# Last chunk's chain into attention reordered, its fold done by two products, and the query side of two chunks moved to GpSimd

## The chip, the cores and the metric

One core of a Trainium2 chip runs the whole program. The metric is device time in microseconds (us) of that core. The engines are TensorE (PE in the profile), VectorE (DVE), ScalarE (ACT), GpSimd (POOL) and SyncE (SP), which here only issues DMAs.

## The reference, cut to what matters

Two transformer layers on x of 2048 tokens by 128 features. The stages around the change are the end of layer 0's mixture of experts and the front of layer 1's attention:

```python
# layer 0 feed-forward: a shared expert and 8 gated ones
x = x + shared + selected
# layer 1 attention, on n = layernorm(x)
q_in = linear(n, Wq, bq);  Q = linear(cat(q_in, conv1d(q_in, convq)), qproj)   # kernel of 3 tokens
k_in = linear(n, Wk, bk);  K = linear(cat(k_in, conv1d(k_in, convk)), kproj)
V = linear(n, Wv, bv)
tau   = sigmoid(conv1x1(gelu(depthwise3(n, tau1)), tau2))
delta = sigmoid(conv1x1(gelu(depthwise3(n, del1)), del2))
scores = einsum(Q, K) / sqrt(8) * tau[..., None] + delta[:, :, None, :]
x = x + linear(softmax(scores) @ V, out_w, out_b)        # 16 heads of 8
# layer 1 feed-forward: 8 experts, each token goes to two of them
```

## The kernel before

The 2048 tokens are cut into four chunks of 512 (`RANGE`, for the convolutions; the last has 513 columns). Layer 0 runs a scan over the chunks, and beside it the feed-forward of chunks 0 to 2. `scan_order` is one order of steps, written by hand, that every engine program walks with its own functions: `epilog`, `gates`, `ffn` (36 up-projections, each with its down-projections), `later` (the norm of layer 1), `kside` (keys and delta), `tside` (the depthwise taps of tau) and `qside` (queries, tau and values). A function yields once a step, and `pull(gen, n)` advances it by n steps; so the order of `pull` calls is the order in each engine's queue.

The feed-forward of chunk 3 is the last. Beside its steps run the key, tau and query sides of chunks 0 to 2, and twenty of the "early" units (`EARLY_STEPS`): a unit is two products of queries with 512 keys into two PSUM banks, and one VectorE reduction of both to maxima. Each gated expert's output goes through `gate_expert` (VectorE, `GO`, L1687), then `add` (GpSimd, `FO += GO`, L2091). After expert 8's `add`, TensorE transposes `FO` (L896), and VectorE adds the result into `x_tok` (L1705). Two pulls of `Q2`, the query side of chunk 2, stand at steps 48 and 50, in front of and behind that fold.

Then comes the chain of chunk 3: statistics (VectorE L1507, L1511), `power` (GpSimd, rstd and shift, L2022 to L2032), the scaling of tokens (`scaled`, ScalarE, L1224), transposes (PE L732), the copy to `XN` (ACT L1361), the keys' convolution (PE L948, L951, ACT L1382, L1385) with the depthwise taps of delta (DVE L1751, L1755) and their Gelu (ACT L1405), the gate products (PE L959, L962) and the sigmoid (ACT L1392, L1393). `parts_of` (DVE L1733 to L1741) splits keys, delta or queries into three bf16 parts. These go out to memory and come back in the layout of the score products: keys over `sk` (SP L2414, L2421), delta over `sc` (`delta_out` L661 and `delta_in` L669, for chunk 3 in ScalarE's queue), queries over `sq` (SP L2443).

The remaining units of group 0's maxima are the `first` units (0 to 11, and one of a single key column; PE L1059 and L1051, DVE L1827). Those over the keys of chunk 3 wait for both the keys and delta to have landed. Their negated maxima (DVE L1823) go through `turned` (PE L1082, ACT L1445, five VectorE instructions L1846 to L1854, SP L2449 and L2453) and become three more rows of the queries. `ahead` does `AHEAD` units of group 1 meanwhile (PE L1074, DVE L1836). `meet` is a barrier of all engines.

Behind it `attention_order` runs 16 groups of 32 score units. A unit has two score products (PE L1110), two exponentials (ACT L1474), one unit of maxima for the next group (PE L1074, DVE L1836), and from the fifth on the eight products with the values (PE L1122). Maxima run `LEAD_MAXIMA` = 10 units ahead of the scores: six are done before the barrier, and four stand in front of the first score. VectorE first does `query_parts(3)` there (L1803, then L1733 to L1741).

Of the kernel before, what the change touches and what calls it, by code (L numbers as in the profile page):

```python
# [16 lines left out]
C = 512  # L17
# [59 lines left out]
def scan_order(p):  # L77
# [52 lines left out]
    Q2 = p["qside"](2)  # L130
    for step, _ in enumerate(chain(p["epilog"](3), both(p["gates"](3), p["ffn"](3)))):
# [6 lines left out]
        if step in (48, 50):  # L138
            pull(Q2)
# [3 lines left out]
    L, K, tau, Q = p["later"](3), p["kside"](3), p["tside"](3), p["qside"](3)  # L143
# [79 lines left out]
def nothing(*_):  # L223
# [8 lines left out]
            kside=lambda c: idle(KSIDE), tside=lambda c: idle(TSIDE), qside=lambda c: idle(QSIDE), early=nothing, first=nothing, ahead=nothing, turned=nothing,  # L232
# [23 lines left out]
EARLY_STEPS = (29, 30, 31, 32, 33, 34, 35, 36, 37, 39, 40, 41, 42, 43, 44, 45, 46, 47, 48, 49)  # L256
EARLY = len(EARLY_STEPS)

AHEAD = 6

FIRST = 13 + AHEAD

# [35 lines left out]
def attention_order(p):  # L298
# [88 lines left out]

    for _ in range(LEAD_MAXIMA - AHEAD):
        next_max()
    for G in range(NG):  # L390
# [5 lines left out]
        for h in range(HALVES):  # L396
# [28 lines left out]
def build(nc, A, out):  # L425
    with ExitStack() as ctx:
# [54 lines left out]
        with ExitStack() as ph:  # L481
# [45 lines left out]
            SQ = [sa(f"SQ{i}", [128, C])[:, :] for i in range(2)]  # L527

            pp2, yy2, vv2 = (pp_, GO[0]), (yy, GO[1]), (vv[:, :], FO[:, :])

            ey, vp = (yy, pp_), (vv[:, :], sa("vv1", [128, C])[:, :])
# [194 lines left out]
        def tensor_program(e):  # L726
# [134 lines left out]
            def ffn(tc):  # L861
# [31 lines left out]
                w.wait_ge(S("gated"), 9 * tc + 9)  # L893
                w.wait_ge(S("ffn_sum"), 8 * tc + 8)
                for b in range(4):
                    t = e.transpose(bank(SUM_BANK[tc])[:, 128 * b:128 * b + 128], FO[:, 128 * b:128 * b + 128], ident[:, :])  # L896
# [69 lines left out]
            def kside(c):  # L966
                made(c)
                w.wait_ge(S("gate_d"), c)
                if c == 3:
                    w.wait_ge(S("f_free"), EARLY)  # L970
# [7 lines left out]
                yield from idle(4)  # L978

# [8 lines left out]
            def qside(c):  # L988
# [7 lines left out]
                elif c == 3:  # L996
                    w.wait_ge(S("x_ffn"), 4)
                conv(c, "convq", 1, 0, "mm_convq")
                yield
                if c != 2:  # L1000
                    values(c)
                    yield from idle(2)
                    w.wait_ge(S("v"), 4 * c + 4)
# [1592 lines left out]
```

## Time and profile before

| | us |
|---|---|
| median of 3 runs | 1483.82 (1479.96 to 1485.55) |
| the profiled execution | 1478.26 |
| its span in the profile | 1476.4 |

PE is busy for 1263.8 us of the span, VectorE for 1231.4, ScalarE for 1034.7 and GpSimd for 662.6. The span is from the first to the last instruction, and what lies around it is 1.9 us. A line of a timeline merges equal instructions that follow each other; "idle before" names what ended the wait. Matmuls of four-byte numbers appear as two instructions each, transposes as one.

### The profile page before, as it was taken

How to read it: one execution, taken by the hardware profiler on the slowest of the kernel's cores; microseconds unless marked ns; L12 is line 12 of the kernel's file. 1: busy time of each engine (PE TensorE's matmuls, PEld its weight loads, DVE VectorE, ACT ScalarE, POOL GpSimd, SP SyncE). 2: the span in 40 equal slices, each digit the busy share in tenths (PEclk: the TensorE clock that was granted, in tenths of full speed). 3: DMA queues.
4: the chain of work that ended last, by engine and by line, in shares of the span. 5: the costliest groups of instructions: out<-in, count | busy, mean ns of one | idle time of the engine just before them, and what ended most of it. 6: DMA issues, size and time to landing. Idle time of an engine off the chain costs nothing.

```text
span 1476.4 us, 22824 instructions
## 1 busy us (share of the span) xinstructions
PE 1263.8 (86%) x8424; PEld 498.1 (34%) x8424; DVE 1231.4 (83%) x1574; ACT 1034.7 (70%) x1832; POOL 662.6 (45%) x762
## 2 busy tenths in 40 slices
PE   4645789888977996887479999999999999999996
PEld 2211334333443443333212222222222222223896
DVE  3999988898989874666689999999999999982764
ACT  5541488678836833643249998999989998998654
POOL 1989878977978864624303001200020003430374
PEclk8767889999988998999669999999999999999999
DMA  8222132212322212430222115100010000002023
GB/s 238 83 77 86 57 95 79 85 60 86 93 71 86 88 29 67 101 90 22 45 65 52 31 31 84 23 3 2 2 24 2 2 2 2 20 28 56 19 76 117
DMA packets 83577, 84.15 MB, mean 57 GB/s; under 512 B 15497, under 2 KB 59018, under 8 KB 83466
## 3 DMA queue, kind: packets, MB, share of 16 engines
q1 hardware_dynamic: 80852, 77.47, 19.5%
q0 software_dynamic: 2496, 5.13, 1.0%
q8 instruction: 66, 1.08, 0.3%
q14 instruction: 45, 0.37, 0.1%
q10 hardware_dynamic: 118, 0.10, 0.0%
HBM read 66.45 MB, written 16.23 MB: 56 GB/s over the span
## 4 chain that ended last, share of the span: by engine, by line
PE 49%; DVE 25%; ACT 9%; issue 8%; POOL 7%; DMA 2%; DVEq 0%; ACTq 0%; POOLq 0%; SPq 0%
DVE mx L1836 14%; PE PS L1122 13%; PE PS L1110 7%; PE PS L858 5%; PE PS L1074 5%; PE PS L867 5%; PE PS L810 2%; POOL D L2060 2%; PE PS L1192 2%; DVE D L1613 2%; PE PS L1207 2%; ACT D L1321 1%; DVE PS L1592 1%; ACT L1321 1%; PE PS L776 1%
## 5 line engine op out<-in xcount | busy, mean ns | idle before, releaser
L1474 ACT ACTIVATE aa<-PS 128x512 f32<-128x512 f32 x1024 | 551.8, 598 | 51.2 <-PE PS L1110 41.0
L1836 DVE TENSOR_REDUCE mx<-PS 128x2 f32<-128x1024 f32 x480 | 551.8, 1216 | 10.2 <-PE PS L1074 8.1
L1122 PE MATMUL PS<-aa,D 128*32 128x256 f32 x4096 | 321.9, 392 | 1.5 <-ACT aa L1474 0.6
L1110 PE MATMUL PS<-D 54*128 54x512 bf16 x1024 | 215.8, 390 | 9.4 <-ACT aa L1474 9.4
L1074 PE MATMUL PS<-D 51*128 51x512 bf16 x960 | 194.2, 387 | 15.6 <-DVE mx L1836 13.0
L2168 POOL CAST n<-nm 16x128 bf16<-16x128 f32 x15 | 4.2, 282 | 409.3 <-ACT nm L1456 409.3
L867 PE MATMUL PS<-xnT,f_w 128*128 128x512 f32 x288 | 159.2, 647 | 7.7 <-ACT HB L1348 6.9
L1592 DVE TENSOR_TENSOR_SCAN PS<-PS,D 128x512 f32<-128x512 f32 x128 | 157.5, 1231 | 7.6
L1348 ACT ACTIVATE HB<-PS 128x512 f32<-128x512 f32 x144 | 84.0, 595 | 106.3 <-PE PS L867 99.2
L858 PE MATMUL PS<-HB,f_w 128*128 128x512 f32 x288 | 147.1, 620 | 6.8 <-DVE GO L1687 5.9
L1122 PEld LDWEIGHTS PS<-aa,D 128*32 128x32 f32 x4096 | 84.3, 108 | 195.3 <-issue 153.4
L1321 ACT ACTIVATE D<-D,Am 128x512 f32<-128x512 f32 x128 | 85.1, 714 | 73.9 <-DVE D L1613 71.9
L810 PE MATMUL PS<-D,ident 128*128 128x512 f32 x192 | 107.9, 687 | 32.7 <-POOL D L2067 27.9
L2067 POOL TENSOR_TENSOR D<-D 128x1024 f32<-128x1024 f32 x48 | 113.0, 2354 | 47.6 <-DVE D L1613 47.5
L1110 PEld LDWEIGHTS PS<-D 54*128 54x128 bf16 x1024 | 54.4, 93 | 221.5 <-ACT aa L1474 165.3
L2060 POOL TENSOR_TENSOR D<-D 128x1024 f32<-128x1024 f32 x48 | 113.2, 2358 | 26.6 <-DVE D L1560 23.4
L1613 DVE TENSOR_TENSOR_SCAN D<-D,hl,PS 128x512 f32<-128x512 f32 x96 | 122.6, 1277 | 2.9
L858 PEld LDWEIGHTS PS<-HB,f_w 128*128 128x128 f32 x288 | 57.0, 199 | 82.7 <-issue 70.5
L2304 POOL DMA_INDIRECT ys<-D,idsI x46 | 48.6, 1056 | 77.5 <-DVE D L1981 70.6
L867 PEld LDWEIGHTS PS<-xnT,f_w 128*128 128x128 f32 x288 | 54.5, 203 | 76.0 <-issue 51.7
L810 PEld LDWEIGHTS PS<-D,ident 128*128 128x128 f32 x192 | 39.3, 212 | 91.4 <-issue 51.1
L1605 DVE SCALAR_TENSOR_TENSOR PS<-PS,D 128x512 f32<-128x512 f32 x96 | 66.8, 695 | 2.6 <-POOL D L2060 0.3
(385 smaller groups left out, 1667.1 us busy)
## 6 DMA issues: line engine op xcount, KB each, us to landing
D<-bc SPq DMA_DIRECT2D x128, 256.0 KB, 3.5
GB<-gd SPq DMA_DIRECT2D x32, 256.0 KB, 4.1
D<-sq SPq DMA_DIRECT2D x8, 384.0 KB, 5.6
xs<-zero SPq DMA_DIRECT2D x1, 2944.0 KB, 18.6
f_w<-in_L_ffn_experts_w SPq DMA_DIRECT2D x1, 2048.0 KB, 9.6
f_w<-in_L_ffn_experts_w SPq DMA_DIRECT2D x8, 256.0 KB, 6.1
aa<-in_L_ffn_W SPq DMA_DIRECT2D x8, 256.0 KB, 3.3
D<-in_L_ffn_W SPq DMA_DIRECT2D x8, 256.0 KB, 3.5
```

The costliest lines, as they stand in the source:

```text
L810: e.matmul(bank(g), ident[:, :], wb[k % 4][:, g, :], start=(n == 0), stop=(n == 15)).then_inc(S("mm_sum"), 1)
L858: e.matmul(down_bank(tc, n // 4), f_w2[:, n // 4, n % 4, :], HB1[i % 6], start=(n % 4 == 0), stop=(n % 4 == 3)).then_inc(S("mm_down"), 1)
L867: e.matmul(bank(4 + i % 2), f_w1[:, n // 4, 128 * (n % 4):128 * (n % 4) + 128], XN[:, ts], start=True, stop=True).then_inc(S("mm_up"), 1)
L1074: t = e.matmul(to[:, hh, :], query(hh, qc % 2, p, b), KS[64 * hh:64 * hh + 51, p, 512 * c:512 * c + 512], start=True, stop=True)
L1110: e.matmul(take_exp(s + hh), KS[64 * hh:64 * hh + 54, p, 128 * kb:128 * kb + 128], QP[64 * hh:64 * hh + 54, qc % 2, p, :], start=True, sto ...
L1122: t = e.matmul(PS[32 * j:32 * j + 32, 7, cs], va[:, kb, 9 * h:9 * h + 32], Pt[K % 3][:, 512 * j + 256 * n:512 * j + 256 * n + 256], start= ...
L1321: e.activation(ab[k % 3][:, g, :], DL[tc % 2][:, g, :], ACT.Exp, scale=Am[:, c:c + 1]).then_inc(S("a"), 1)
L1474: e.activation(Pt[K % 3][:, c:c + 512], bank((s + hh) % 3), ACT.Exp).then_inc(S("e_free"), 1)
L1592: e.tensor_tensor_scan(out=bank(3), data0=bank(2), data1=ab[k % 3][:, g, :], initial=0.0, op0=ALU.max, op1=ALU.mult).then_inc(S("sP"), 1)
L1613: e.tensor_tensor_scan(out=pb[k % 2][:, g, :], data0=ab[k % 3][:, g, :], data1=bank(3), initial=hl[:, 16 * g + n:16 * g + n + 1] if tc els ...
L1836: e.tensor_reduce(mx4[:, G % 2, :, pair, b, c:c + 1], max_banks(m), AX.X, ALU.max).then_inc(freed(m)[0], 1)
L2060: e.tensor_tensor(wb[k % 4], DU[tc % 2][:, :, :], Bb[k % 3].unsqueeze(1).to_broadcast([128, 2, C]), ALU.mult).then_inc(S("wB"), 1)
```

## The change

- Fold: for chunk 3 the last `add` is gone. TensorE multiplies `FO` (which holds experts 0 to 7) and then `GO[0]` (expert 8) by the identity, both into one bank.
- Norm of chunk 3: GpSimd makes rstd alone, and VectorE subtracts and scales in place of ScalarE.
- Order: the query side of chunk 2 leaves the feed-forward's steps and is spread over the chain of chunk 3 (`third`). Early units are 18, at steps 29 to 46, and the `first` units are 15.
- Keys and delta of chunk 3 (`keys`): the Gelu comes before the evacuation of the convolution, both depthwise taps before the parts, and no `first` unit stands between the parts of the keys and those of delta. GpSimd's taps for tau wait until the parts of delta are done. Each key part goes out as soon as it is made; of the keys that come back, the first two of eight rows of heads (`0:2`) come first, and the other six (`2:8`) once delta has gone out.
- `query_parts` of chunks 2 and 3 are now GpSimd's `last`, behind the barrier; so are their DMAs.
- `AHEAD` is 4; the other six units of the lead are spread over the first six score units. A one-column exponential on ScalarE stands at the barrier.

```diff
     drain(sgen)
     p["collect"](3)
-    Q2 = p["qside"](2)
...
-        if step in (48, 50):
-            pull(Q2)
...
     drain(lgen)
-    L, K, tau, Q = p["later"](3), p["kside"](3), p["tside"](3), p["qside"](3)
+    p["third"]("gelu")
...
+    L = p["later"](3)
     pull(L)
-    pull(Q2)
-    pull(L, 3)
-    pull(Q2)
+    p["third"]("conv")
     drain(L)
-    drain(Q2)
-    pull(K, 2)
-    drain(tau)
-    pull(Q)
-    pull(K)
+    for stage in ("conv", "taps", "gelu", "evac", "gate"):
+        p["keys"](stage)
+    p["third"]("gate")
+    p["third"]("values")
+    for stage in ("parts", "out", "delta", "rest"):
+        p["keys"](stage)
+    drain(p["tside"](3))
+    p["third"]("sums")
     firsts(0, 1)
-    pull(K, 2)
-    pull(Q)
-    firsts(2, 3)
-    drain(K)
-    pull(Q)
-    firsts(4, 5, 6)
-    pull(Q)
-    firsts(7, 8, 9, 10, 11)
-    drain(Q)
-    firsts(12)
+    p["queries"]("conv")
+    firsts(2, 3, 4, 5)
+    p["queries"]("values")
+    p["queries"]("gelu")
+    firsts(6, 7, 8, 9)
+    p["queries"]("gate0")
+    firsts(10, 11)
+    p["queries"]("gate1")
+    firsts(12, 13, 14)
     ahead(0)
     p["turned"]()
     ahead(*range(1, AHEAD))
...
-AHEAD = 6
+AHEAD = 4
...
-    for _ in range(LEAD_MAXIMA - AHEAD):
-        next_max()
...
             next_max()
+            if unit["max"] < t + 1 + LEAD_MAXIMA:
+                next_max()
...
# TensorE, ffn(3): the fold
+                if tc == 3:
+                    w.wait_ge(S("hid"), 144)
+                    for x, (summed, sem, n) in enumerate(((FO, "ffn_sum", 31), (GO[0], "gated", 36))):
+                        w.wait_ge(S(sem), n)
+                        for b in range(4):
+                            t = e.matmul(bank(4)[:, 128 * b:128 * b + 128], summed[:, 128 * b:128 * b + 128], ident[:, :],
+                                         start=(x == 0 and b == 0), stop=(x == 1 and b == 3))
...
# VectorE, later(3)
+                    drain(norm(7, 3, 4, "p"))
+                    w.wait_ge(S("p_tp"), 7)
+                    w.wait_ge(S("p_pw"), 23)
+                    for b in range(4):
+                        e.tensor_scalar(xn1[:, b, :], x_tok[:, 12 + b, :], mv[:, 4 + b, 0:1], rstd[:, 4 + b:5 + b],
+                                        ALU.subtract, ALU.mult).then_inc(S("p_xn"), 1)
...
# ScalarE
+                elif stage == "delta":
+                    delta_out(e, w, 3)
+                    delta_in(e, w, 3)
...
# GpSimd, tside: taps of tau
                     if c == 3:
-                        w.wait_ge(S("t1"), 24)
+                        w.wait_ge(S("d_parts"), 20)
...
+            def last():
+                for c, src, tau, n in ((2, q2, tau2, C), (3, C3[0], tauC, C + 1)):
+                    out_ = [qp[:, k, 0:n] for k in range(3)]
...
+                    e.tensor_scalar(src, src, float(8.0 ** -0.5), None, ALU.mult).then_inc(tau_done, 1)
+                    e.tensor_tensor(src, src, tau, ALU.mult).then_inc(tau_done, 1)
+                    w.wait_ge(S("d_sq"), 48 * c)
+                    e.tensor_copy(out_[0], src).then_inc(done, 1)
+                    e.tensor_tensor(src, src, out_[0], ALU.subtract).then_inc(done, 1)
+                    e.tensor_copy(out_[1], src).then_inc(done, 1)
+                    e.tensor_tensor(src, src, out_[1], ALU.subtract).then_inc(done, 1)
+                    e.tensor_copy(out_[2], src).then_inc(done, 1)
...
# SyncE
+            def keys(stage):
+                if stage == "out":
+                    for k, g, m in ((0, 0, 3), (1, 3, 2), (2, 5, 1)):
+                        w.wait_ge(S("k_parts"), 16 + 2 * k)
...
+                    for hh in range(2):
+                        e.dma_start(KS[64 * hh:64 * hh + 48, 0:2, a:b], rows48(sk, hh, slice(a, b))[:, 0:2]).then_inc(
+                            S("d_key3"), 16)
+                elif stage == "rest":
+                    w.wait_ge(S("d_sd"), 64)
+                    w.wait_ge(S("d_key2"), KEY_ROWS)
+                    for hh in range(2):
+                        e.dma_start(KS[64 * hh:64 * hh + 48, 2:8, a:b], rows48(sk, hh, slice(a, b))[:, 2:8]).then_inc(
+                            S("d_key2"), 16)
...
             def last():
+                query_out(2)
                 query_out(3)
```

The waits inside `last` between its own instructions are left out above. The memsets of the value tiles of chunks 2 and 3 move from `qside(2)` to `qside(1)` on GpSimd, and one transpose of `turned` goes to bank 2.

## Rows read from the trace of the kernel before

**Rows 1.** Windows: us, busy us of each engine (count), granted clock, DMA share, GB/s.

```profile
754.00:760.00 6.00, 5.04 (x18) 1.10 (x18) 5.21 (x6) 5.89 (x11) 0.00 (x0) 0.50 0.76 219
760.00:766.00 6.00, 6.00 (x42) 1.05 (x43) 4.13 (x4) 3.04 (x7) 0.00 (x0) 0.51 0.16 46
1100.00:1200.00 100.00, 97.20 (x1028) 25.62 (x1026) 99.00 (x94) 93.30 (x175) 3.36 (x10) 1.00 0.05 6
```

**Rows 2.** Timeline of PE: start us, us, line, operation, [idle before].

```profile
680.71 1.98 PE L858 MATMUL PS<-HB,f_w 128*128 128x512 f32 x4
682.53 2.74 PE L948 MATMUL PS<-xnT,w_convq 128*128 128x512 f32 x6
...
688.94 0.63 PE L896 MATMUL PS<-ident,FO 128*128 128x128 f32 x4 [1.64 <-POOL FO L2091]
...
692.07 1.16 PE L984 MATMUL PS<-w_Wv,xnT 128*128 128x128 f32 x8 [0.78 <-ACT D L1393]
...
753.33 0.63 PE L1110 MATMUL PS<-D 54*128 54x512 bf16 x2
...
761.99 1.08 PE L1122 MATMUL PS<-aa,D 128*32 128x256 f32 x8
...
763.97 1.08 PE L1122 MATMUL PS<-aa,D 128*32 128x256 f32 x8
```

**Rows 3.** Timeline of DVE, same columns.

```profile
686.78 0.68 DVE L1687 SCALAR_TENSOR_TENSOR GO<-PS,GB 128x512 f32<-128x512 f32 x1
...
691.24 0.38 DVE L1511 BATCH_NORM_AGGREGATE mv<-st 128x2 f32<-128x6 f32 x4
...
738.10 0.24 DVE L1823 TENSOR_REDUCE mxh<-mx 128x16 f32<-128x80 f32 x1
...
741.08 5.73 DVE L1836 TENSOR_REDUCE mx<-PS 128x2 f32<-128x1024 f32 x5
...
747.79 0.43 DVE L1733 CAST D<-D 128x513 bf16<-128x513 f32 x1
...
750.18 0.43 DVE L1741 CAST D<-D 128x513 bf16<-128x513 f32 x1
...
764.08 1.23 DVE L1836 TENSOR_REDUCE mx<-PS 128x2 f32<-128x1024 f32 x1 [0.75 <-PE PS L1074]
```

**Rows 4.** Timeline of POOL.

```profile
687.54 1.26 POOL L2091 TENSOR_TENSOR FO<-FO,GO 128x512 f32<-128x512 f32 x1 [6.75 <-DVE GO L1687]
...
692.34 1.38 POOL L2028 TENSOR_TENSOR rstd<-rstd,mhalf 128x4 f32<-128x4 f32 x1
```

**Rows 5.** Chain that ended last, 690 to 730 us: start us, us, what.

```profile
694.09 1.66 ACT xn L1224 x4
...
697.60 4.54 PE PS L948 x6
...
702.89 0.69 ACT D L1385
...
704.80 1.22 DVE D L1737
...
714.42 6.13 DMA sc<-D
...
721.95 2.89 DMA D<-sc
...
727.51 3.71 PE PS L959 x4
```

**Rows 6.** Groups of DVE by line: busy us, mean ns.

```profile
L1893 DVE TENSOR_SCALAR xn<-x_tok,mv,rstd 128x128 f32<-128x128 f32 x8 | 2.2, 372 | 0.5 <-POOL rstd L2028 0.5
```

**Rows 7.** One line, L661: from issue to landing over its four issues.

```profile
DMA to landing us min/median/max: 3.2/4.5/6.1
```

**Rows 8.** Timeline of the SP queue.

```profile
742.58 0.57 SPq L2453 DMA_DIRECT2D D<-nd  x2
```

**Rows 9.** Groups of POOL by line.

```profile
L2137 POOL TENSOR_SCALAR D<-xnT,t1w 128x512 f32<-128x512 f32 (+2 forms) x16 | 26.3, 1642 | 1.6
```

More of the change, by code:

```diff
@@ L231 @@
             ffn=lambda tc: idle(FFN), later=lambda tc: idle(NORM), combine=lambda: idle(COMBINE), start=nothing,
-            kside=lambda c: idle(KSIDE), tside=lambda c: idle(TSIDE), qside=lambda c: idle(QSIDE), early=nothing, first=nothing, ahead=nothing, turned=nothing,
+            kside=lambda c: idle(KSIDE), tside=lambda c: idle(TSIDE), qside=lambda c: idle(QSIDE), early=nothing, first=nothing, ahead=nothing, turned=nothing, keys=nothing, queries=nothing, third=nothing,
             rows=nothing, mulW=nothing, mulB=nothing, scanX=nothing, scanP=nothing, mulC=nothing, clamp=nothing,
@@ new lines, in queries @@
+            def queries(stage):
+                if stage == "conv":
+                    w.wait_ge(S("mm_convq"), 4)
+                    w.wait_ge(S("q_parts"), 10)
+                    conv(3, 0, 1, 7, "conv_q")
+                elif stage == "gelu":
+                    for g in range(2):
+                        w.wait_ge(S("t2"), 5 * g + 35)
+                        e.activation(TC[g], TC[g], ACT.Gelu).then_inc(S("gelu_t"), 1)
+                elif stage == "gate1":
+                    w.wait_ge(S("mm_gate_t"), 4)
+                    w.wait_ge(S("q_tau"), 2)
+                    gate(3, tauC, 128, cols[:, 6:7], 1, 0, "gate_t")
@@ L1434, in qside @@
                 yield
-                if c != 2:
-                    gelus()
-                    yield from idle(2)
+                for g in range(2):
+                    w.wait_ge(S("t2"), 10 * c + 5 * g + 5)
+                    e.activation(TC[g][:, 0:b - a], TC[g][:, 0:b - a], ACT.Gelu).then_inc(S("gelu_t"), 1)
+                yield from idle(2)
                 w.wait_ge(S("mm_gate_t"), c + 1)
@@ L1784, in qside, with keys, third, queries @@
                 yield from idle(3)
-                if c < 3:
-                    query_parts(c)
+                query_parts(c)
                 yield
                 yield
+            def keys(stage):
+                if stage == "taps":
+                    w.wait_ge(S("mm_gate_d"), 3)
+                    taps(3, 0)
+                    taps(3, 1)
+                elif stage == "parts":
+                    w.wait_ge(S("conv_k"), 4)
+                    w.wait_ge(S("d_sk"), 144)
+                    parts_of(C3[1], kp, C + 1, S("k_parts"), 15)
+                elif stage == "delta":
+                    w.wait_ge(S("gate_d"), 4)
+                    w.wait_ge(S("d_sd"), 48)
+                    parts_of(delC, dp, C + 1, S("d_parts"), 15)
+            def third(stage):
+                if stage == "sums":
+                    values(2)
+            def queries(stage):
+                if stage == "values":
+                    values(3)
             def values(c):
@@ L1857, in vector_program @@
                                    epilog=epilog, gates=gates, ffn=ffn, later=later, combine=combine, kside=kside, qside=qside,
-                                   early=early, first=first, ahead=lambda j, m: maxima(1, j, m), turned=turned))
+                                   early=early, first=first, ahead=lambda j, m: maxima(1, j, m), turned=turned, keys=keys,
+                                   queries=queries, third=third))
             meet(e, w)
@@ L1868, in turn @@
                 w.wait_ge(S("m_full"), m + 1)
+                w.wait_ge(S("rs"), 1)
                 if G:
@@ L2101, in ffn @@
                 yield
-                add(8)
+                if tc < 3:
+                    add(8)
                 yield
```

204 lines of the change are left out of this document (136 added, 68 removed).

## The prediction

> **What bounds the kernel now.** I read the windows of the attention stage first. Far from its edges VectorE is busy for 99.0 of 100 us and TensorE for 97.2 [rows 1]: both are full, TensorE takes new maxima only when VectorE has freed a bank, and nothing in this change touches a unit there. So the stage keeps its length once it runs, and a gain or a loss must arise before its steady part, or in its first score units. I then read the timelines of PE, DVE and POOL at the end of the last feed-forward [rows 2 to 4], because the fold is the one door between the layers, and then the chain that ended last from there to the first score [rows 5]. The reader is to see that this stretch is no throughput problem. It is one chain of hand-overs, from the last down-projection (ends 682.69) to the first score (753.33) [rows 2], 70.6 us, and beside it VectorE does side work. I follow it by its marks, and end at 766.0, where the clock comes up (0.51 in the window before, 1.00 later) [rows 1], with seven score units and seventeen maxima done: six ahead and eleven reductions behind the barrier, the last ending at 765.31 [rows 3]. The changed kernel passes through the same state (ten ahead), so the distance to it is the gain.
>
> **The change part by part, on the clock of the profiled execution.**
>
> *Fold.* Before, the down-projections end at 682.69, then comes the query convolution of chunk 2 (2.74), two early units, `GO` at 686.78, the `add` (1.26) and the transposes, which end at 689.57 [rows 2 to 4]. After, none of this stands in between: `GO` starts about 683.0 (0.3 for the early unit that now stands at step 38) and ends at 683.7, the products of `FO` run beside it, and the four products of `GO` cost what four such products cost for the values, 1.16 [rows 2]. End 684.9: gain 4.65. If step 38 also waits for VectorE, 0.7 less.
>
> *Norm.* From the last statistics (691.62) [rows 3] to the end of the scaling (695.75) [rows 5] it is 4.13. After: rstd 1.38 [rows 4] and one small instruction with its hand-over, 0.4, since shift falls away, then four scalings on VectorE. Eight of them elsewhere took 2.2 [rows 6], so 1.1. Sum 2.9, gain 1.2. The convolution for queries (2.74) now fills TensorE beside it: it ends near 687.7, before the tokens are ready at 684.9 + 0.75 + 1.3 + 2.9, about 689.9, so it is covered; uncovered it would cost 2.7.
>
> *Keys and delta.* From the start of the keys' convolution (697.60) to delta's parts done (714.42) it is 16.8, with the end of the evacuation at 703.58 [rows 5]. Two reductions (2.3, at 1.15 each by five in 5.73 [rows 3]) stand between the two sets of parts, and the parts run beside GpSimd's taps: a cast that takes 0.43 alone took 1.22 [rows 3, 5]. After, the convolution and its evacuation are again 6.0, two sets of parts alone are 2 x 2.82 (747.79 to 750.61 [rows 3]), sum 11.65. The Gelu before the evacuation is ready by about 5, since both taps end 4 us in, and the sigmoid is covered by the keys' parts. Gain 5.1. That assumes the lower clock for the convolution again, 4.54 against 2.74 for the same six instructions [rows 2, 5]. Here TensorE stands still for some 2.4 us between the query convolution and the transposes, and before it fell after such a gap. The Trainium skill, "TensorE: Matmul & The Clock Gate", section "Why this matters for your kernels", tells one to avoid longer idle gaps between bursts, and would let a gap of this size pass. By that the convolution would be at 2.4 GHz, 1.8 shorter. The Gelu would then end last and leave 0.6 of it, so I add nothing.
>
> *Delta to memory and back.* Before 10.4, from 714.42 to landed at 724.84, of which 6.13 is the way out and 2.89 the last way in [rows 5]. After, the way out meets less traffic: its four issues took 3.2 to 6.1, median 4.5 [rows 7]. I take 4.5, then 1.3 for the first issue in ScalarE's queue (720.6 to 721.95), then 2.9. But the six remaining rows of the keys now leave from SP on the same semaphore and share the DMA engines with delta; I give them 1.5, between 0 and the 2.9 of one more such transfer. Sum 10.2, gain 0.2, with 8.7 to 13.2 as bounds. Queued behind `delta_in` on ScalarE is the evacuation of chunk 3's queries, which so comes some 2 us after its product; the four `first` units that need no new key cover it on VectorE (4.6).
>
> *First units.* From landing (724.84) to the negated maxima (738.34) it is 13.5 [rows 3, 5]: eight units (9.2), one small, and TensorE's tau product at the lower clock in their way (3.71). After, again eight units and a small one behind the landing; the two more units of this stage, and the adds of the values, lie in front of it. The gate is cut in two halves of 1.9 at the lower clock, each behind a unit in flight; GpSimd's taps, which now start only after delta's parts and take 13.3, end 3 us behind the landing and the second half waits for them, covered by six units (6.9). I leave 1.0 of stall (0 to 3). 11.5, gain 2.0.
>
> *To the steady state.* Before, 738.34 to 766.0 is 27.7. It held six units ahead, `query_parts(3)` (3.5 on VectorE, TensorE's maxima behind it), four units in front of the first score, and the table load for the exponential. After: the rows of `turned` leave for the queries 4.5 us after the negated maxima (742.85 for the second [rows 8]) and land in an estimated 2.9, as delta's did; three units ahead are done sooner, so the first score starts 7.4 us behind the maxima. Then four score units with two maxima each, VectorE-bound, 4 x 2.30; two with products of the values at the lower clock, 1.98 (761.99 to 763.97 [rows 2]) and 0.6 for the second maxima; one of 1.98: 16.4. Sum 23.8, gain 3.9 (2 to 6).
>
> *Covered parts.* `last` on GpSimd: fourteen instructions, at most 1.64 each [rows 9], 23 us, and some 5 for the wait until chunk 2's parts are out. SP's `query_out`, the first expert weights and then group 1's rows queue behind it; these are wanted only a whole group after the barrier, some 37 us (32 units of 1.15), so 9 us are to spare. What it shares with VectorE: the maxima read PSUM, and the five reductions at 741.08 and those before are at the same 1.15, so I take nothing. ScalarE's one-column exponential lies where ScalarE waits for the first score, and takes the table load with it. The two pairs of memsets move to another place where GpSimd has time. Both are nothing.
>
> Sum: 4.65 + 1.2 + 5.1 + 0.2 + 2.0 + 3.9 = 17.05. The profiled execution took 1478.3, so 1461.2; the median of the runs is 5.5 above it, so 1466.8, rounded to **1467**.
>
> **The rivals.**
> *Delta lands late.* ScalarE issues `delta_in` behind SP's two large transfers. If these go first, landing takes 13 instead of 10 us, and if the gate's second half then also stalls for 3, the gain is 12: 1472. For it: delta's way out took 6.13 beside the keys' transfers. Against: the transfer is smaller now. By the Trainium skill, "Trainium Kernel Development and Optimization", section "Key Constraints", DMAs of all queues run on the same 16 engines and interleave. That is why ScalarE's own queue protects nothing.
> *The clock stays low.* This is the slower one. In the first score units VectorE paces TensorE, at about 1.8 busy of 2.3 us, and at 0.84 busy (754 to 760) the clock stayed at 0.50 [rows 1]. Each unit at the lower clock costs 1.98 against 1.15, 0.83 more. It eats 17 us from 21 units on and is slower by over 0.5% (7.4) from 30. At 30: 1492. Against it: as soon as the products of the values run, TensorE is the bound and busy throughout (6.00 of 6), after which the clock rose.
> *The front is not what sets the end.* If later work (weights, the next rows behind GpSimd's `last`) takes the gain back, say 12 of 17, the time is 1479. Against it: the 9 us to spare.
> *More than summed.* Clock high from fold to keys, delta in 8.7, no stall: 22 gained, 1462 and down.
>
> **How the numbers follow.** 0.5% (7.4 us) is about what a measurement of this kernel can tell from no change. My forecast with gains of 14 to 21: 0.60. Smaller gains, down to 7.5: 0.20. More than 21: 0.07. Within 0.5%: 0.09. Slower: 0.04. Faster 0.87, same 0.09, slower 0.04. The range 1460 to 1477 leaves some 0.17 out, on both sides. The likeliest case's own range is 1463 to 1473.
>
> **What would show it.** In the changed profile: the fold ends 2.2 us behind the last down-projection; the second cast of the parts (L1737 before) takes 0.43 and not 1.22; delta's parts are done 11.7 behind the start of the keys' convolution, and land 10 behind that; the first score starts some 50 us behind the last down-projection instead of 70.6, and the steady state comes 16.4 behind it; the groups of attention keep their period. I am wrong if the clock stays at 0.5 past the seventh score unit, if GpSimd's `last` delays SP, or if the groups become longer.

## The result and the profile after

The changed kernel took 1460.95 us (median of six runs, 1458.26 to 1468.75) against 1482.53 for the kernel before: ratio 0.9858, 95% interval 0.9829 to 0.9886. I had said 1467, with a range of 1460 to 1477, and faster with 0.87. A second measurement on another chip gave 1465.62 (1460.72 to 1470.52) against 1478.71: 0.9894, interval 0.9868 to 0.9921. The median of the first lies 6 below the forecast, that of the second 1.4 below. The medians of the first are 21.6 apart, those of the second 13.1.

The profiled execution took 1459.42 (span 1457.6) against 1478.26: 18.84 less, where my sum said 17.05. First the windows of the changed kernel, columns as in [rows 1].

```profile
0.00:70.00 70.00, 37.42 (x101) 17.48 (x101) 43.95 (x64) 37.31 (x57) 34.52 (x52) 0.80 0.55 160
...
688.30:691.80 3.50, 0.68 (x5) 0.42 (x4) 1.11 (x4) 1.28 (x2) 0.94 (x1) 0.91 0.00 0
691.80:698.30 6.50, 6.44 (x13) 3.33 (x14) 4.02 (x6) 1.27 (x3) 0.00 (x0) 0.52 0.00 0
698.30:704.70 6.40, 5.50 (x24) 2.22 (x24) 5.23 (x11) 3.64 (x6) 0.00 (x0) 1.00 0.39 126
731.80:745.90 14.10, 11.19 (x52) 2.04 (x52) 12.57 (x12) 6.65 (x13) 10.64 (x11) 0.50 0.19 58
...
745.90:765.30 19.40, 19.40 (x220) 5.70 (x220) 19.34 (x18) 17.68 (x33) 2.87 (x4) 1.00 0.43 123
...
1100.00:1200.00 100.00, 97.89 (x1040) 25.46 (x1032) 98.95 (x93) 93.61 (x177) 5.06 (x15) 1.00 0.01 2
```

The steady part is what it was in [rows 1]: VectorE 98.95 of 100, TensorE 97.89. The change lies in front of it. The timeline of PE answers to [rows 2]:

```profile
681.49 2.31 PE L860 MATMUL PS<-HB,f_w 128*128 128x512 f32 x5
683.64 1.05 PE L900 MATMUL PS<-ident,FO 128*128 128x128 f32 x8
684.58 1.16 PE L900 MATMUL PS<-ident,GO 128*128 128x128 f32 x8
685.58 2.74 PE L959 MATMUL PS<-xnT,w_convq 128*128 128x512 f32 x6
690.51 0.66 PE L734 MATMUL PS<-ident,xn 128*128 128x128 f32 x4 [2.19 <-DVE xn L1801]
691.86 5.49 PE L959 MATMUL PS<-xnT,w_convk 128*128 128x512 f32 x6 [0.69 <-ACT xnT L1411]
...
714.31 0.96 PE L1106 MATMUL PS<-D 51*128 51x512 bf16 x4
...
731.76 0.61 PE L1159 MATMUL PS<-D 54*128 54x512 bf16 x2 [1.71 <-DVEq L620]
```

That of DVE answers to [rows 3]:

```profile
683.84 0.69 DVE L1770 SCALAR_TENSOR_TENSOR GO<-PS,GB 128x512 f32<-128x512 f32 x1 [3.24 <-PE PS L860]
...
689.35 1.11 DVE L1801 TENSOR_SCALAR xn<-x_tok,mv,rstd 128x128 f32<-128x128 f32 x4 [1.56 <-POOL rstd L2223]
...
699.19 0.43 DVE L1825 CAST D<-D 128x513 bf16<-128x513 f32 x1 [3.12 <-ACT D L1435]
...
700.39 0.43 DVE L1829 CAST D<-D 128x513 bf16<-128x513 f32 x1
...
704.25 0.42 DVE L1833 CAST D<-D 16x513 bf16<-16x513 f32 x1
...
709.29 4.62 DVE L1933 TENSOR_REDUCE mx<-PS 128x2 f32<-128x1024 f32 x4 [1.56 <-PE PS L1106]
714.36 0.88 DVE L1900 TENSOR_TENSOR D<-PS,bb 128x128 f32<-128x128 f32 x4 [0.45 <-PE PS L1040]
715.16 4.61 DVE L1933 TENSOR_REDUCE mx<-PS 128x2 f32<-128x1024 f32 x4
720.20 2.36 DVE L1933 TENSOR_REDUCE mx<-PS 128x2 f32<-128x1024 f32 x2 [0.44 <-PE PS L1106]
722.79 2.36 DVE L1933 TENSOR_REDUCE mx<-PS 128x2 f32<-128x1024 f32 x2 [0.23 <-PE PS L1106]
...
725.27 0.24 DVE L1929 TENSOR_REDUCE mxh<-mx 128x16 f32<-128x80 f32 x1
...
732.90 11.40 DVE L1942 TENSOR_REDUCE mx<-PS 128x2 f32<-128x1024 f32 x10 [1.25 <-PE PS L1123]
744.73 20.61 DVE L1942 TENSOR_REDUCE mx<-PS 128x2 f32<-128x1024 f32 x18 [0.42 <-PE PS L1123]
```

POOL, for [rows 4] and for `last`:

```profile
688.20 1.04 POOL L2223 TENSOR_TENSOR rstd<-rstd,mhalf 128x4 f32<-128x4 f32 x1
...
731.80 1.50 POOL L2285 TENSOR_SCALAR SQ<-SQ 128x512 f32<-128x512 f32 x1 [13.85 <-DVEq L620]
...
748.37 0.61 POOL L2298 CAST D<-D 128x513 bf16<-128x513 f32 x1
```

ScalarE's queue, for delta's way [rows 5, 7]:

```profile
704.71 0.37 ACTq L663 DMA_DIRECT2D sc<-D  x1
706.62 2.02 ACTq L671 DMA_DIRECT2D D<-sc  x2
```

Both kernels can be set against each other at the same marks (us). The negated maxima of the first group count at their end (L1823 before, L1929 after), those of the next group at their start (L1842 before, L1948 after); by then the steady part runs.

| from, to | before | after | gain |
|---|---|---|---|
| start to last down-projection | 682.69 | 683.80 | -1.11 |
| to end of fold | 6.88 | 1.94 | 4.94 |
| to keys' convolution | 8.03 | 6.12 | 1.91 |
| to delta's parts done | 16.79 | 12.81 | 3.98 |
| to negated maxima (end) | 23.95 | 20.84 | 3.11 |
| to negated maxima of the next group (start) | 45.36 | 39.89 | 5.47 |
| 14 groups more | 537.8 | 537.9 | -0.1 |
| to the end | 154.9 | 154.3 | 0.6 |

Of the first line 0.86 was there already at 638, where the two kernels do the same; the other 0.25 I put down to the early unit at step 38.

### The profile page after: what moved, and what is told of

The parts are those of the page before. It is cut to its first block, busy times and chain, and to the rows that moved or that the text cites. A ratio compares the mean times of both kernels' runs of the same rounds, so it can differ in the third digit from the quotient of the medians.

```text
span 1457.6 us, 22845 instructions
## 1 busy us (share of the span) xinstructions
PE 1263.3 (87%) x8436; PEld 502.6 (34%) x8436; DVE 1223.8 (84%) x1566; ACT 1031.2 (71%) x1827; POOL 674.1 (46%) x773
## 4 chain that ended last, share of the span: by engine, by line
PE 50%; DVE 25%; ACT 9%; issue 8%; POOL 7%; DMA 1%; DVEq 0%; POOLq 0%; SPq 0%; ACTq 0%
DVE mx L1942 14%; PE PS L1171 13%; PE PS L1159 7%; PE PS L860 5%; PE PS L869 5%; PE PS L1123 5%; PE PS L812 3%; POOL D L2168 2%; PE PS L1241 2%; PE PS L1256 2%; DVE D L1696 1%; ACT D L1370 1%; DVE PS L1675 1%; ACT L1370 1%; PE PS L778 1%
## 5 line engine op out<-in xcount | busy, mean ns | idle before, releaser
L1159 PE MATMUL PS<-D 54*128 54x512 bf16 x1024 | 214.0, 389 | 10.2 <-ACT aa L1557 8.5
L812 PEld LDWEIGHTS PS<-D,ident 128*128 128x128 f32 x192 | 39.3, 212 | 89.7 <-issue 50.2
```

Of the source, the lines that this page charges most:

```text
L812: e.matmul(bank(g), ident[:, :], wb[k % 4][:, g, :], start=(n == 0), stop=(n == 15)).then_inc(S("mm_sum"), 1)
L1159: e.matmul(take_exp(s + hh), KS[64 * hh:64 * hh + 54, p, 128 * kb:128 * kb + 128], QP[64 * hh:64 * hh + 54, qc % 2, p, :], start=True, sto ...
```

## The experiments

All are edits of the changed kernel, and each has one execution unless it says otherwise. Chips and executions differ: the kernel before ran at 1490.45 beside the first four, at 1482.85 beside the next four, at 1478.71 (median of 11) beside the repeat and the two runs about the order, at 1494.40 beside the last. So totals decide little, and I compare spans between marks. These are the marks, measured from the end of the fold; "takes" is the keys' convolution with its single columns, "first part" is the start of the first cast, and the last column is from the negated maxima of the first group to those of the next.

| run | total us | keys' conv starts | takes | first part | delta's parts | negated maxima | first score | next group |
|---|---|---|---|---|---|---|---|---|
| changed kernel | 1459.42 | 6.12 | 6.42 | 13.45 | 18.93 | 39.77 | 46.02 | 39.9 |
| again | 1470.52 | 6.11 | 6.45 | 13.47 | 18.95 | 40.40 | 46.72 | 41.2 |
| last add back | 1472.48 | 6.40 | 6.07 | 13.39 | 18.87 | 41.08 | 47.39 | 40.6 |
| query conv. in front | 1472.79 | 6.58 | 5.02 | 12.51 | 17.99 | 39.98 | 46.08 | 40.1 |
| parts on VectorE | 1475.68 | 6.12 | 6.42 | 13.44 | 18.93 | 41.49 | 47.82 | 44.1 |
| six units in front | 1476.42 | 6.12 | 3.40 | 11.76 | 17.24 | 40.22 | 52.35 | 40.8 |
| taps beside parts | 1470.28 | 6.11 | 6.44 | 13.46 | 19.82 | 41.48 | 47.81 | 40.6 |
| keys at once | 1462.09 | 6.11 | 4.88 | 11.90 | 17.38 | 39.04 | 45.15 | 40.2 |
| gap filled | 1462.11 | 6.12 | 3.40 | 11.76 | 17.24 | 39.00 | 45.09 | 40.2 |
| filled, Gelu later | 1462.82 | 6.12 | 3.40 | 10.43 | 15.92 | 38.34 | 44.67 | 40.5 |
| Gelu later | 1462.02 | 6.11 | 4.86 | 11.89 | 17.37 | 39.22 | 45.33 | 40.2 |
| filled, Gelu later, two in front | 1462.15 | 6.11 | 3.41 | 10.43 | 15.92 | 38.36 | 45.50 | 40.8 |
| delta out twice | 1473.88 | 6.11 | 6.42 | 13.44 | 18.93 | 42.31 | 48.42 | 40.2 |

**The changed kernel again** (six executions).

> The changed kernel itself, beside the next two on the same chip. Every theory expects the ratio of the first timing, 0.983 to 0.989, some 1461 us, and the marks of the first profile within 0.3: from the end of the fold 6.1 to the keys' convolution, 13.4 to the first part, 39.8 to the negated maxima, 46.0 to the first score, 79.7 to the negated maxima of the next group. If the last stretch of the program (154 us behind the last group) differs by several us from one chip to another, it will differ here for all kernels alike.

The ratio was 0.9894 and the median 1465.62, so the expected range and the expected 1461 were both missed by a little. Up to the first score the marks hold to 0.7, not to the 0.3 I had said. The next group's came 81.6 behind the fold and not 79.7: TensorE's clock rose later, and VectorE waited 0.56, 0.20 and 0.17 more for it. And in this execution the last down-projection ended at 691.69 and not at 683.80. Its first window shows a granted clock of 0.73, where the first profile had 0.80:

```profile
0.00:70.00 70.00, 39.45 (x95) 19.05 (x96) 41.81 (x62) 35.96 (x55) 32.47 (x50) 0.73 0.57 160
```

Between these two executions, 7.9 of the 11.1 thus arose in layer 0, in front of the change. The spread bounds what a total can tell: 12 between the fastest and the slowest execution of the changed kernel, over both measurements.

**Last add back** (the fold as before).

```diff
-                if tc == 3:
-                    w.wait_ge(S("hid"), 144)
...
+                    for b in range(4):
+                        t = e.transpose(bank(4)[:, 128 * b:128 * b + 128], FO[:, 128 * b:128 * b + 128], ident[:, :])
```

> The changed kernel with the old fold: GpSimd adds expert 8 and TensorE transposes FO alone, with no query convolution or early unit in front of it. Theory (most of the fold's gain is that nothing stands between the last down-projection and the gating of expert 8): the fold ends 0.8 us later than in the changed kernel, 2.75 us behind the last down-projection instead of 1.94, and not 6.9 as before the change. Rival (the two products are what saved the 4.7 us): it ends more than 3 us later. In the span: +0.8 against +3 or more.

```profile
685.51 0.63 PE L900 MATMUL PS<-ident,FO 128*128 128x128 f32 x4 [2.21 <-POOL FO L2198]
```

TensorE waits 2.21 for GpSimd, and the fold ends 2.84 behind the last down-projection in place of 1.94. The two products are worth 0.90.

**Query convolution in front of the fold.**

```diff
+        if step == 48:
+            p["third"]("conv")
...
     pull(L)
-    p["third"]("conv")
```

> The changed kernel with chunk 2's query convolution at step 48, behind the last down-projections and in front of the fold. Theory (the chain through the fold counts one to one): the fold ends 2.7 to 2.9 us later, as long as the convolution is (2.74), and each later mark with it; the keys' convolution starts 2.8 later. Rival (the chain has slack behind the fold, in statistics and hand-overs): the first score comes less than 1 us later.

The fold ends 4.35 behind the last down-projection: 2.41 more, nearly the 2.74 of the convolution, and from the fold to the keys' convolution nothing is won back (6.58 against 6.12). Counted from the last down-projection, the first score comes 2.5 later than in the first profile and 1.8 later than in the second, so the rival (less than 1) is out. With the 0.90 that is 3.3 of the fold's 4.94. The rest I put down to the two early units and what they wait for; no run tests it.

**Parts of chunk 2's queries back on VectorE.**

```diff
-                for c, src, tau, n in ((2, q2, tau2, C), (3, C3[0], tauC, C + 1)):
+                for c, src, tau, n in ((3, C3[0], tauC, C + 1),):
...
+            def last():   # VectorE, in front of the remaining maxima
+                e.scalar_tensor_tensor(out=q2, in0=q2, scalar=float(8.0 ** -0.5), in1=tau2, op0=ALU.mult, op1=ALU.mult)
+                parts_of(q2, qp, C, S("q_parts"), 10)
```

> The changed kernel with the parts of chunk 2's queries back on VectorE, behind the barrier; those of chunk 3 stay on GpSimd. Theory (VectorE's work before the steady state counts one to one, but for the 1.25 us in which it now waits for TensorE there): the first group's negated maxima come 3.5 - 1.25 = 2.3 us later, measured from the barrier. Rival (the work is hidden while TensorE is at its lower clock): 0 to 0.5 us.

The ten reductions that follow started 11.12 behind the negated maxima, against 7.39 and 7.46 in the two profiles of the changed kernel: 3.7 lost there, where I expected 2.3, and the rival (hidden anyway) is out. At the next group's maxima it is 2.9 to 4.2, since the clock rose at different moments in the two profiles. Timeline of DVE in this run:

```profile
733.43 0.69 DVE L2110 SCALAR_TENSOR_TENSOR SQ<-SQ,vv 128x512 f32<-128x512 f32 x1 [0.25 <-DVEq L620]
...
734.62 0.98 DVE L1827 TENSOR_TENSOR SQ<-SQ,D 128x512 f32<-128x512 f32 x1
735.63 0.59 DVE L1829 CAST D<-SQ 128x512 bf16<-128x512 f32 x1
736.26 1.45 DVE L1831 TENSOR_TENSOR SQ<-SQ,D 128x512 f32<-128x512 f32 x1
```

The same subtraction takes 0.98 and 1.45 beside GpSimd's two first instructions (734.32 to 737.17), and 0.69 alone. The six instructions take 4.66 until the next reduction, in place of 3.46 for the same work in the kernel before (747.06 to 750.52), and then VectorE has all its maxima still to do. The Trainium skill, "SBUF — State Buffer", section "SBUF: two separate sides", says that VectorE, when both its inputs lie in SBUF, and an instruction of GpSimd that reads SBUF shut each other out for a whole instruction. For the subtraction, whose inputs both lie in SBUF, the direction agrees. The reductions read PSUM, and the ten of them beside GpSimd's `last` took 11.40 in the changed kernel, 1.14 each, as without it.

**Six units in front of the first score, as before.**

```diff
+    for _ in range(6):
+        next_max()
     for G in range(NG):
```

> The changed kernel with the six units of maxima of the lead in front of the first score instead of two to a score unit. VectorE has the same work. Theory (score units with products of the values run at the lower clock, 1.98 us each, and they should start at once so that VectorE's lead covers them): the first score 6 to 7 us later, and the first group's negated maxima 1.5 to 3 us later. Rival (only VectorE's count of reductions matters): negated maxima within 0.5 us, though the first score comes 6 us later.

The first score comes 5.9 later (12.13 behind the negated maxima against 6.25), but the next group's maxima only 0.9 later than in the first profile, and 0.4 earlier than in the second. It lies between theory and rival, and nearer the rival: the place of the six units in the queue is worth 1 at most. VectorE has the same reductions to do either way.

**GpSimd's taps released earlier.**

```diff
                     if c == 3:
-                        w.wait_ge(S("d_parts"), 20)
+                        w.wait_ge(S("t1"), 24)
```

> The changed kernel with GpSimd's taps of tau for chunk 3 released by VectorE's taps, as before, and not by the parts of delta, so that both engines work in SBUF side by side. Theory (the two engines block each other there): the second cast and second subtraction of the parts slow down again, from 0.43 and 0.69 to about 1.2 and 1.1, both sets of parts end 2 to 3 us later than in the changed kernel (704.7 measured from the same start), and so do the first units; the gate of tau no longer stalls them, which gives back 0.7. Span +1.5 to +2.5. Rival (no effect on each other, the old slow casts had another cause): parts unchanged, span -0.5.

The parts took 6.36 in place of 5.48, so 0.9. That is in the theory's direction but less than half of its 2 to 3. Only the last three instructions were slowed: the taps did not start before 707.7, since their tile was still being read by the gate products of chunk 2. In this order the overlap of the kernel before can't come back in full; the wait on `d_parts` is worth 0.9 at the end of the parts. Nothing was given back at the gate: VectorE stood idle for 1.21 and 0.83 behind its halves.

**All the keys' rows in front of delta.**

```diff
-                    w.wait_ge(S("d_sd"), 64)
                     w.wait_ge(S("d_key2"), KEY_ROWS)
```

> The changed kernel with the other six rows of heads of the last keys fetched at once behind the first two, without waiting until delta has gone out. Theory (in the changed kernel delta lands some 4 us before VectorE comes to the units that need it): delta goes out slower, by 1 to 3 us, and nothing else moves, span within 0.3 us by the marks. Rival (the landing of delta sets the first units): the units over the last keys start 1 to 3 us later.

From delta's parts to the negated maxima it took 21.66, against 20.84 and 21.45 in the two runs of the changed kernel: nothing gained and nothing lost that could be told from their spread. The order of keys and delta in the DMA engines does move delta: here it had landed at most 6.20 behind the first issue of its return (8.65 behind its parts), where the six runs in which TensorE waited for it had 7.3 to 7.9 (9.3 to 10.2). Its way out was 0.5 slower, where 1 to 3 were expected. But VectorE was at earlier work and made nothing of it. Its convolution took 4.88 with nothing changed in front of it: the moment at which the clock comes back differs from one execution to the next.

**TensorE's gap filled.**

```diff
                     conv(2, "convq", 1, 0, "mm_convq")
+                    for _ in range(2):
+                        e.matmul(bank(0), ident[:, :], XN[:, 0:C], start=True, stop=True)
```

> The changed kernel with two extra products of the identity by 512 columns into a free bank behind chunk 2's query convolution, so that TensorE stands still for 0.5 us instead of 2.2 before the transposes; their result is not used. Theory (the keys' convolution ran at 1.2 GHz because of that gap): it now takes 2.7 instead of 5.5 us and its single columns 0.6 instead of 1.0, the Gelu then ends last, and the parts start 1.5 us sooner; every later mark moves by -1.5. Rival (the clock falls anyway in the 0.7 us of transposes and the gaps around them): nothing moves.

The two products write a bank that nobody reads. Timeline of PE and, below, the window of the convolution:

```profile
688.17 1.88 PE L1011 MATMUL PS<-xnT,ident 128*128 128x512 f32 x4
690.53 0.66 PE L734 MATMUL PS<-ident,xn 128*128 128x128 f32 x4 [0.48 <-DVE xn L1803]
691.88 2.84 PE L959 MATMUL PS<-xnT,w_convk 128*128 128x512 f32 x6 [0.69 <-ACT xnT L1413]
...
712.37 1.04 PE L1108 MATMUL PS<-D 51*128 51x512 bf16 x4 [0.86 <-DMA D<-sc]
```

```profile
691.90:695.30 3.40, 3.40 (x13) 1.94 (x14) 3.26 (x5) 0.64 (x1) 0.00 (x0) 1.00 0.00 0
```

With 0.48 of idleness in front of the transposes and not 2.19 the clock stays at 1.00, and the convolution takes 2.84 and not 5.49. The first part comes 1.7 earlier, not 3.0, since the second Gelu now stands in front of the evacuation. At the negated maxima 0.8 to 1.4 is left of it. TensorE now waits 0.86 for delta's return, but VectorE does not: its reduction over the new keys starts at 713.02, right behind the sums. What is lost against the first profile is idleness behind the tau gate at the lower clock, as in the next run.

**The same, with the second Gelu behind the evacuation.**

```diff
+                    conv(3, 1, K_BANK[3], 7, "conv_k")
+                    w.wait_ge(S("t1"), 24)
+                    e.activation(TC[3], TC[3], ACT.Gelu).then_inc(S("gelu_d"), 1)
```

> As the run before with the extra products, and on ScalarE the evacuation of the keys' convolution stands between the two Gelus instead of behind both. Theory: the parts of the keys follow VectorE's taps at once, 2.8 to 3.1 us sooner than in the changed kernel, and later marks move by -2.8. Rival (then the sigmoid of delta, which still waits for the second Gelu, is the later one): -1.5 at most behind the parts of delta.

The first part comes at 10.43: 3.0 gained. But 1.4 to 2.1 is left at the negated maxima, and 0.8 at the next group's against the first profile. In the way are the tau gate's products at the lower clock (2.07 and 0.42 a half, VectorE idle 1.21 and 0.83 behind them, against 1.52 and 1.79 with 0.44 and 0.23 in the changed kernel).

**The order of the Gelu alone** (the edit just shown, without the two products).

> The second Gelu behind the evacuation of the keys' convolution, without the two filling products. Theory, that it is the convolution at the lower clock that sets the first part: ScalarE is done with both Gelus before the convolution's last column, so the order is worth nothing here: first part 13.4 behind the end of the fold as in the changed kernel (within 0.2), and delta's parts 0 to 0.7 later. Rival, that the order alone carries the 1.3 which it gave on top of the filling: first part at 12.1.

The first part came at 11.89, and taken by itself the rival looks right. But the convolution took 4.86 here, 1.56 less, and the first part came 1.56 earlier. The run above in which the Gelu stood in its old place had the same convolution (4.88) and its first part at 11.90. So at this clock the order is worth nothing, as the theory said, and 1.33 (11.76 to 10.43) once the convolution runs at 1.00.

**Filled, Gelu later, two units in front of the first score** (six executions).

```diff
+    for _ in range(2):
+        next_max()
     for G in range(NG):
```

> TensorE's gap filled with two more products (they write a bank that nobody reads), the second Gelu behind the evacuation, and two of the six units of lead back in front of the first score. Theory: in the changed kernel VectorE stands idle for 1.25 us in front of the first score, because the next unit of maxima is queued on TensorE behind the score product, which waits for the queries' transfer. With two units in front, VectorE runs through: from the negated maxima to those of the next group 39.3 in place of the 40.5 that the same kernel without these two units took (39.9 in the changed kernel), so 3.0 less at the first part, 1.4 less at the negated maxima and 2.0 to 2.6 less at the next group's, all from the end of the fold. By the total, 0.998 of the changed kernel, which a median can hardly tell from it. Rival, that the first score's place in the queue sets the rate and not VectorE: the two units delay the first score by 1 to 2, and the next group's maxima are not earlier (40.5 or more).

1466.50 (1462.15 to 1469.60), ratio to the kernel before 0.9907, interval 0.9883 to 0.9932: no better than the changed kernel's 0.9894 on the same chip. By the marks the rival is right. The first score comes 0.8 later, and the next group's maxima take 40.8, not 39.3. Timeline of DVE:

```profile
733.65 12.54 DVE L1947 TENSOR_REDUCE mx<-PS 128x2 f32<-128x1024 f32 x11 [0.82 <-PE PS L1127]
746.61 1.23 DVE L1947 TENSOR_REDUCE mx<-PS 128x2 f32<-128x1024 f32 x1 [0.42 <-PE PS L1127]
748.59 8.01 DVE L1947 TENSOR_REDUCE mx<-PS 128x2 f32<-128x1024 f32 x7 [0.76 <-PE PS L1127]
```

0.43 of idleness in front of the first score is saved (0.82 for 1.25), but a second unit with products of the values now falls in the time at the lower clock and costs 0.76. The clock rose 22 us behind the negated maxima, and 20.4 in the changed kernel.

**Delta out twice.**

```diff
                     delta_out(e, w, 3)
+                    w.wait_ge(S("d_sd"), 64)
+                    e.dma_start(sc[0:48, RANGE[3][0]:RANGE[3][1]].rearrange("(k h) t -> h k t", k=3),
+                                dp[:, :, 0:C + 1]).then_inc(S("d_sd"), 16)
+                    w.wait_ge(S("d_sd"), 80)
                     delta_in(e, w, 3)
```

> Delta's parts are written out to memory twice, one after the other, before they come back, so that delta lands later and nothing else changes. Theory: in the changed kernel the landing does not set the first units over the new keys; VectorE is at earlier units and at the sums of the values until 715.2, and TensorE's first product over the new keys starts 9.6 behind delta's parts. The landing has about 1.5 of slack. The second write costs about 1.9, so the first new unit comes 0.3 to 0.8 later (its reduction 10.8 to 11.3 behind delta's parts, against 10.5 to 10.6), with TensorE waiting for the transfer, and the negated maxima at 21.2 to 22.5 (20.8 and 21.5 in the two runs of the changed kernel). The rival, my prediction's own step, that the landing sets the first units: everything from there shifts by the full 1.9 or more, the first new unit at 12.4, the negated maxima at 22.8 to 23.4.

ScalarE's queue, then PE:

```profile
707.83 0.36 ACTq L1479 DMA_DIRECT2D sc<-D  x1
711.56 2.02 ACTq L671 DMA_DIRECT2D D<-sc  x2
```

```profile
714.58 2.08 PE L1040 MATMUL PS<-w_Wv,xnT 128*128 128x128 f32 x8 [1.12 <-ACT D L1435]
716.59 1.04 PE L1106 MATMUL PS<-D 51*128 51x512 bf16 x4
```

The second write took 3.73, twice what I had taken, so delta's return was issued 3.8 later. The first new unit came at 11.67 behind delta's parts, only 1.0 to 1.2 later. That does not measure the slack of the landing, because the return was itself shorter here: at most 5.03 from its first issue to TensorE's first product over the new keys (716.59), which did not wait for it. What TensorE waited for was the evacuation of chunk 3's queries, which stands behind `delta_in` in ScalarE's queue. The negated maxima came 1.9 to 2.5 later: the delay also pushed the tau gate into time at the lower clock.

The landing shows in the second profile of the changed kernel, PE and then DVE:

```profile
722.58 1.03 PE L1106 MATMUL PS<-D 51*128 51x512 bf16 x4 [0.34 <-DMA D<-sc]
```

```profile
722.27 0.88 DVE L1900 TENSOR_TENSOR D<-PS,bb 128x128 f32<-128x128 f32 x4 [0.45 <-PE PS L1040]
723.22 4.62 DVE L1933 TENSOR_REDUCE mx<-PS 128x2 f32<-128x1024 f32 x4
```

Delta landed 9.99 behind its parts, TensorE waited 0.34 for it, and VectorE stood idle for 0.07. TensorE waited for it in five more runs too (query convolution in front 1.09, parts on VectorE 0.54, taps beside 0.80, gap filled 0.86, Gelu later 0.82), and VectorE then stood idle for 0.27 at most. So the landing and VectorE's own work end together, to some tenths. In the first profile TensorE did not wait for it. An estimate: had the return taken 7.3 to 7.7 there (it can't have been longer, the first product over the new keys started at 714.31), its slack was 0.2 to 0.6, since a reduction started 0.65 behind the landing in the runs in which VectorE waited for it.

## Why the prediction was right, and where its terms were off

The mechanism was right: one chain from the fold to the steady part shortened, the groups keep their period (537.9 against 537.8), `last` is done at 748.98 and delays nothing, and the clock is up at 745.9. What the runs undo and so show are the products of the fold, the place of the query convolution, chunk 2's query parts on GpSimd, the wait on `d_parts` and the order of the lead. The norm, the keys' and delta's parts without units between them, and the one-column exponential were not undone; their shares are read from the marks alone. Point by point:

*Fold.* 4.65 was said; 4.94 measured to the end of the fold, 4.69 net of the early unit. The fold ends 1.94 behind the last down-projection, where 2.2 was said. Shown by two runs, for 3.3 of it.

*Norm.* 1.2 was said, 1.91 measured. `power` took 1.04 where I took [rows 4]'s 1.38. From the last statistics (687.79) to the end of the scaling (690.46) it is 2.67, not 2.9. From there to the keys' convolution it is 1.40, where it was 1.85.

*Keys and delta.* 5.1 was said, 3.98 measured: the one term that fell short. The casts are at 0.43, as said, so the parts gave what was expected. The convolution was mis-sized: I took 6.0 to the end of the evacuation, by [rows 5], where a part of it ran at the higher clock. Here all of it was at 0.52, 5.49 and the single columns to 698.28, and the evacuation ended at 699.16: 7.3. The filled gap shows the cause, in that the idleness was replaced by products; whether the shorter gap or the added work kept the clock, no run separates. The Trainium skill's section that I weighed there ("TensorE: Matmul & The Clock Gate", "Why this matters for your kernels") would have let the gap of 2.19 pass. It did not hold: of nine runs with a gap of 2.2 eight had part or all of the convolution at the lower clock, and all three filled ones had none. The ninth (six units in front, 2.20) kept the clock too; why is open. I had said that the Gelu would leave 0.6 of a faster convolution; it left 1.7, since more was lost to the clock than I had taken.

*Delta to memory and back, first units.* 0.2 and 2.0 were said, 3.11 measured for both. The sum was near, and two errors in it cancel. The way out took 1.9 (I took 4.5 from [rows 7]); the way in, by the six runs that waited for it, 7.3 to 7.9 from the first issue, where I had 4.2 and 1.5 for the keys beside it. Delta landed 9.99 behind its parts in the second profile and at most 9.64 behind them in the first, where 10.2 was said. I also let the landing alone set the first units. But behind delta's parts VectorE had two sums of values and six units to do, with 1.56 and 0.45 of waiting for TensorE between them, until 715.24, and in the first profile that set the first new unit (10.5). In the second the landing did, by 0.07. With all the keys' rows in front, delta landed at least 0.8 earlier than in the run with the same convolution (8.65 against 9.48), and from its parts to the negated maxima it took 21.66 against 21.85. That the two fell together to some tenths was not in my working. The stall at the gate was 0.67, where I left 1.0, and the taps were not waited for.

*To the steady state.* 3.9 was said. To the seventeenth maxima it is 4.3 by the timelines, and 1.2 came behind them: I had called the two states the same, but the kernel before still waited for TensorE there (0.76, 0.21 and 0.17), while the changed one ran 18 reductions in 20.61 without a gap. Timeline of DVE in the kernel before:

```profile
766.06 6.88 DVE L1836 TENSOR_REDUCE mx<-PS 128x2 f32<-128x1024 f32 x6 [0.76 <-PE PS L1074]
773.15 9.14 DVE L1836 TENSOR_REDUCE mx<-PS 128x2 f32<-128x1024 f32 x8 [0.21 <-PE PS L1074]
```

These 1.2 were luck: nothing in my sum led to them, and in the second profile the changed kernel waited there as well (0.56, 0.20 and 0.17).

The first score came 6.25 behind the maxima, where 7.4 was said. Moving chunk 2's query parts off VectorE is shown as worth 3.7 in this place, and 2.9 to 4.2 at the next group's maxima; the order of the lead is worth 0.4 less to 0.9 more.

The sum of terms was 17.05; by the marks it was 19.2 net of the early unit, less 0.86 from layer 0, plus 0.5 behind: 18.84 in the profile. So the sum accounts for 1.8 of the 6 by which the median lay below the forecast. The other 4 come from the step behind it: I put the median 5.5 above the profiled execution, as before the change, and it lay 1.5 above it (1460.95 against 1459.42).

By the medians' gain, 21.6, the first measurement falls under *more than summed*, to which I gave 0.07, and its median lies below the likeliest case's own range, which began at 1463. The mechanism of that rival did not come: the clock was low in the keys' convolution, delta took more than 8.7 by every run that waited for it, and there was a stall. By mechanism the other rivals did not come either. *Delta lands late*: it landed 9.99 behind its parts in the second profile, at most 9.64 in the first, and not 13. *The clock stays low*: it did through the sixth score unit, and that cost 0.42 of waiting (0.98 in the second profile, where the rise came later), since VectorE ran full at 1.14 a unit (11.40 for ten). *The front is not what sets the end*: every mark kept its lead to the end. The second measurement gave 13.1 of gain and not 21.6; with 12 between executions of one kernel, no mark of the change explains that difference, and it stays open.

## What to carry to other kernels

When a chain is shortened, ask at each mark what the other engines still owe there: delta's return and VectorE's own work between two marks (six units and two sums) ended within some tenths of each other, and landing the one earlier gained nothing that showed. When a transfer is delayed to test its slack, check whether it still takes as long: here it was issued 3.8 later and came at most 1.5 later. A term at half clock is to be bounded with its whole length at half clock, and a filler of 1.9 us in the gap before it is a cheap test. A gain at an early mark (3.0) can be down to 0.8 three marks later, so measure at the mark in front of the steady part, and not at the edit.

## What the runs showed of the hardware that I had not expected

- A gap of 2.19 in front of TensorE's products, and the granted clock was at 0.52 for 6.5 us behind it; with 0.48 it stayed at 1.00 in all three filled runs, and with the gap in one of nine. With the gap the same convolution took 3.40 once, 4.86 to 4.88, or 6.07 to 6.45, with its single columns: the moment of the rise differs between executions.
- The same 48 KB write took 1.97 to its semaphore, and 3.73 when it was repeated beside the two transfers of 289 KB with the keys' other rows. Delta's return (twice 24 KB) took 7.3 to 7.9 from its first issue beside them, and at most 6.20 when they had been issued ahead of it.
- VectorE's subtraction of 128x512 took 0.69 alone, and 0.98 to 1.45 beside GpSimd, while reductions from PSUM stayed at 1.14.
